# Weight casts of a feed-forward block moved from VectorE to GpSimd, on the queue that also issues the weight loads

## The reference

```python
def attn(x, Wq, Wk, Wv, Wo, gamma, beta):        # 16 heads of 64, causal
    q, k, v = projections of x
    out = softmax(mask(q @ k.T / 8)) @ v
    y = x + out @ Wo
    return layernorm(y, eps=1e-3) * gamma + beta
def ffn(x, w_gate, w_up, w_down):                # DIM 1024, HIDDEN 3072
    wg, wu, wd = w_gate / 127, w_up / 127, w_down / 127
    return (silu(x @ wg.T) * (x @ wu.T)) @ wd.T
x = x + attn(layernorm(x), ...)
x = x + ffn(layernorm(x), ...)                   # x: (16, 2048, 1024) float32
```

## Time and profile before

| what | us |
|---|---|
| median of 3 runs | 4214.85 (4174.06 to 4262.39) |
| time of the profiled execution | 4175.83 |
| its span, slowest core (core 3) | 4174.3 |
| spans of the 8 cores | 4146.8 to 4174.3 |
| mean granted TensorE clock of the cores | 0.839 to 0.845 of full speed |

### The profile page before, as it was taken

How to read it: one execution, slowest core, us unless ns; L and a number is a source line. 1 busy time by engine, 2 the same in 40 slices (tenths; PEclk the granted TensorE clock), 3 DMA queues, 4 the chain that set the end, 5 groups by cost and what they waited for, 6 DMA issues and landing times.

```text
span 4174.3 us, 44886 instructions; the slowest of 8 cores (4146.8 to 4174.3 us)
## 1 busy us (share of the span) xinstructions
PE 2608.2 (62%) x14352; PEld 1122.1 (27%) x14352; DVE 1751.8 (42%) x3199; ACT 1091.5 (26%) x1408; POOL 379.9 (9%) x644
## 2 busy tenths in 40 slices
PE   1455555587857567587714466465878574766877
PEld 0122222233323223233301223132333231332322
DVE  2533455444432441544435334544443325324543
ACT  0210325220036257110012103151100461661100
POOL 0000000022200000022300000000222000001222
PEclk6697678799979789799957976697999796898999
DMA  5102000076630000177741120001676200002776
GB/s 148 43 12 81 25 0 1 11 232 232 232 101 1 0 11 1 51 219 241 233 137 43 37 80 1 0 11 36 224 235 227 76 1 1 11 1 75 226 231 209
DMA packets 125732, 389.81 MB, mean 93 GB/s; under 512 B 14528, under 2 KB 14656, under 8 KB 125504
## 3 DMA queue, kind: packets, MB, share of 16 engines
q0 software_dynamic: 88064, 318.81, 23.4%
q1 hardware_dynamic: 37440, 68.12, 5.5%
HBM read 370.10 MB, written 16.78 MB: 93 GB/s over the span
## 4 chain that ended last, share of the span: by engine, by line
PE 27%; DMA 24%; DVE 21%; ACT 14%; issue 11%; SPq 1%; DVEq 1%; POOL 1%; ACTq 0%; POOLq 0%
ACT zr L711 9%; DMA wstag<-wu 8%; DMA wstag<-wd 6%; DMA wstag<-wg 5%; PE ps L588 3%; PE ps L520 3%; PE ps L326 2%; PE ps L693 2%; PE ps L770 2%; PE ps L476 2%; PE ps L666 2%; PE ps L957 2%; DMA xh<-x 2%; DVE zr L719 1%; PE ps L904 1%
## 5 line engine op out<-in xcount | busy, mean ns | idle before, releaser
L901 PE MATMUL ps<-zr,wgbb 128*128 128x512 bf16 x1536 | 601.3, 391 | 140.6 <-DVE wgbb L827 140.3
L711 ACT ACTIVATE zr<-ps,bbias 128x1024 bf16<-128x1024 f32 (+1 forms) x592 | 618.0, 1060 | 259.4 <-PE ps L696 212.2
L904 PE MATMUL ps<-zr,wubb 128*128 128x512 bf16 x1536 | 599.0, 390 | 109.1 <-DVE wubb L829 106.4
L666 PE MATMUL ps<-zr,vb 128*64 128x512 bf16 (+3 forms) x1280 | 378.4, 366 | 240.1 <-DVE zr L719 153.6
L818 POOL DMA_DIRECT2D wstag<-wu x192 | 119.2, 621 | 3142.0 <-DVE wgbb L827 3095.4
L957 PE MATMUL ps<-zr,wdbb 128*128 128x512 bf16 x1536 | 357.0, 386 | 74.1 <-DVE wdbb L948 72.3
L911 ACT ACTIVATE xst<-ps 128x512 bf16<-128x512 f32 x192 | 114.2, 597 | 1013.0 <-PE ps L901 878.0
L696 PE MATMUL ps<-qsb,kb 128*64 128x512 bf16 (+3 forms) x1280 | 371.5, 376 | 0.0
L693 PE MATMUL ps<-qsb,kb 128*64 128x512 bf16 (+3 forms) x1280 | 369.4, 374 | 0.0
L672 PE MATMUL ps<-zr,cbt 128*64 128x512 bf16 (+3 forms) x1280 | 358.4, 377 | 0.0
L719 DVE TENSOR_TENSOR zr<-zr,cbt 128x128 bf16<-128x128 bf16 x512 | 115.1, 225 | 485.0 <-ACT zr L711 414.5
(11 more groups left out here) (103 smaller groups left out, 3778.7 us busy)
## 6 DMA issues: line engine op xcount, KB each, us to landing
wstag<-wg POOLq DMA_DIRECT2D x192, 512.0 KB, 5.0
wstag<-wu POOLq DMA_DIRECT2D x192, 512.0 KB, 4.9
wstag<-wd POOLq DMA_DIRECT2D x192, 512.0 KB, 4.9
xh<-x SPq DMA_DIRECT2D x128, 256.0 KB, 6.9
o<-xh POOLq DMA_DIRECT2D x64, 256.0 KB, 3.4
tsc<-wk SPq DMA_DIRECT2D x32, 256.0 KB, 2.9
tsc<-wv SPq DMA_DIRECT2D x32, 256.0 KB, 2.7
tsc<-wq SPq DMA_DIRECT2D x32, 256.0 KB, 2.8
```

The costliest lines, as they stand in the source:

```text
L666: w=vsl, p=pap, st=first_av[ar0], tp=av_tp: t.matmul(d, w, p, start=st, stop=False, tile_position=tp, skip_group_check=True),
L711: E_("s", lambda s, d=pap, a=PSB[tslot2][:, 0:512 + n], b=bb: s.activation(d, a, ACT.Exp, bias=b, scale=0.125), reads=[bPS[2 * tslot2], bP ...
L901: E_("t", lambda t, dc=dc, w=wgsl, z=z3_ap[dc], d=PS[gB][:]: t.matmul(d, w, z, start=(dc == 0), stop=(dc == NDC - 1)), reads=[bWG[wsl], z3 ...
L904: E_("t", lambda t, dc=dc, w=wusl, z=z3_ap[dc], d=PS[uB][:]: t.matmul(d, w, z, start=(dc == 0), stop=(dc == NDC - 1)), reads=[bWU[wsl], z3 ...
```

## The change

All three casts go from VectorE's queue to GpSimd's. Shapes, buffers, order of recording and everything else stay. The lambdas of the down cast keep the name v for the engine they get.

```diff
@@ emit_guw_cast
-                    E_("v", lambda v, d=gb_, s=wstag[:, gsl * 1024:(gsl + 1) * 1024]: v.tensor_copy(d, s),
+                    E_("g", lambda g, d=gb_, s=wstag[:, gsl * 1024:(gsl + 1) * 1024]: g.tensor_copy(d, s),
                        reads=[bWST[gsl]], writes=[bWG[wsl]])
-                    E_("v", lambda v, d=ub_, s=wstag[:, usl * 1024:(usl + 1) * 1024]: v.tensor_copy(d, s),
+                    E_("g", lambda g, d=ub_, s=wstag[:, usl * 1024:(usl + 1) * 1024]: g.tensor_copy(d, s),
                        reads=[bWST[usl]], writes=[bWU[wsl]])
@@ down phase
-                        E_("v", lambda v, d=db_, a=stg: v.tensor_scalar(
+                        E_("g", lambda g, d=db_, a=stg: g.tensor_scalar(
                             d, a, 1.0 / 127.0, 0.0, AluOpType.mult, AluOpType.add),
                             reads=[bWST[sl], bCF], writes=[bWD[wsl]])
```

## The result

| | before | after |
|---|---|---|
| median, us | 4180.64 (4168.38 to 4274.58, 10 runs) | 4599.7 (4583.63 to 4623.81, 9 runs) |
| span of the profiled execution | 4174.3 (core 3) | 4597.8 (core 2) |
| spans of the cores | 4146.8 to 4174.3 | 4567.7 to 4597.8 |

The ratio of after to before is 1.1006, 95% interval 1.0983 to 1.103: the change costs 10%, some 420 us. The forecast was 13%, 4765 us in a range of 4590 to 5150; the measured time lies just inside its lower end. In some executions of every kernel here the cores of one half of the chip show a lower granted clock and the time is some per cent longer; such executions are in the medians and not in the ratios.

What follows compares the result with a forecast made beforehand. It took the three-slot ring of loads and casts to bound gate, up and down phases. Added: tf0 200, tf1 294, down 63, edges 15, together 572 over 4175.8, giving 4748, plus 17 for spread: 4765 us, range 4590 to 5150.

Steps and rivals of the forecast that it cites:

- The mechanism: Gate and up: casts waiting for tiles stand ahead of the next step's loads on GpSimd's queue, so loads lose their lead.
- The period: Gate and up: one step of two tiles takes 7.56 us, a sum along GpSimd's queue, against 4.4 measured before.
- The 0.50 from the end of cast u to the next issue: Gate and up: GpSimd issues the next load 0.50 us after cast u is done, one term of the period.
- landing of u: Gate and up: the load of wu takes 5.0 us from issue to landing, one term of the period.
- X: Duration of one cast on GpSimd, taken as 1.3 us, between a low end of 0.695 and a high end of 2.7.
- tf0 passes: Gate and up in tf0: 7.5 us, then 19 periods, 151.1 together; 50 more per pass, 200 for four.
- The down phase: Three loads stay ahead; cast and issue share GpSimd, 2.45 us per step against 2.11, 63 us more in all.
- TensorE's low clock: Gate and up: clock falls to 0.62, a step takes 6.8 us, hidden below 7.56 except 15 us at pass ends.
- The lock between VectorE and GpSimd: tf0 down phases: 16 normalizing VectorE instructions could hold up GpSimd casts, 11 us per pass, 44 in all, left in range.
- The slow cast: Rival: GpSimd's cast becomes the bound, X of 2 or more; about 5160 us at 2.1, 5470 at 2.7. Chance 0.22.
- Shorter landings: Rival: with less traffic u lands after 4.3 us, X is 1.0, period 6.8; about 4580 us. Chance 0.15.
- That GpSimd keeps its lead: Rival: loads issued in time despite casts, gate and up stays at 4.4 us per step, 4123 us total. Chance 0.03.

Runs made afterwards that it cites:

- e3: Against the changed kernel, only the load order differs: the load of tile n + 3 right behind the cast of tile n. 4238.43 us, ratio to before 1.0143.
- e4: Against the kernel before, casts still on VectorE, a step's loads wait for the second cast of the step before. Median 4691.45 us.
- e5: Against the changed kernel, each gate and up cast is done twice on GpSimd. 4968.22 us, ratio 1.1902.
- e2: Against the kernel before, only the down casts move to GpSimd. 4187.12 us, ratio 1.0029.
- e6: Against the changed kernel, weight loads are issued from SyncE, all casts staying on GpSimd. 4043.2 us, ratio to before 0.9687.
- e9: Against the kernel before, weight loads are issued from SyncE, casts staying on VectorE. Median 4087.52 us, ratio 0.9755.
- e1: Against the changed kernel, down casts are back on VectorE, so only gate and up casts are on GpSimd. 4571.95 us, ratio to before 1.0941.
- e8: Against the kernel before, loads convert int32 to bf16 themselves into a ring of 12 bf16 tiles, with no casts. 3924.73 us, ratio 0.9346.

## Why the prediction was right, and its terms

**The mechanism** was as put: the loads lose their lead in gate and up, the down phase keeps it, the period is a sum along GpSimd's queue. e3 and e4 show it from both sides, since the order alone takes the loss away and gives it without the change.

**The period** was forecast at 7.56 us and is 6.74 to 6.85 in the four tf1 passes. The step that failed is the sum 0.50 + 0.61 + landing of u + 0.16 + X (6.27 + X, not 6.26), in two terms:

- The 0.50 from the end of cast u to the next issue isn't there: cast u ends at 1126.20 and load g has started at 1126.15 by the rows above. I took it from the earlier trace rows, where it is the time from VectorE's cast to GpSimd's issue. In the new order load g waits for no cast of the pair just done: its slot was freed by the cast of wu one step earlier. The half microsecond does come back where a load waits for the cast right ahead of it, 0.56 in e3 and in the down phase.
- X was taken as 1.3 and is 1.05, ScalarE's rate for 1024 columns in the earlier trace rows, not that of L913. The Trainium skill ("GPSIMD Engine Reference", section 4.1) calls one-input operations roughly line-rate, by the prediction's estimate 0.85 us, and that is nearer to the measured 1.05 than the 1.54 from the 1.8 cycles of its section 3.1.

The rest held: issue to issue 0.53 (0.61 forecast), landing of wu 5.0 at the median (5.0), landing to cast 0.2 (0.16). With the measured values 0.53 + 5.0 + 0.2 + 1.04 = 6.77. Put in place of 7.56 it takes 0.79 x 168 = 133 from the sum of 572, the down phase another 35 and the edges 14, which leaves 390 against 397 measured in the passes.

**How much of the hit is luck.** With the right terms the passes give 182 us less than the forecast, and 27 us outside them, which no term of the prediction holds, bring the time back: without them it would be about 4573, below the range. So the mechanism was right, the size of the loss was forecast 1.4 times too large, and that the time falls just inside the range is partly luck. Of the signs, GpSimd's casts (1.05 us, not 1.1 to 1.6), the distance of cast u to cast u (6.7 to 6.9, not 7.0 to 8.1), the traffic (153 GB/s, not near 140) and VectorE's busy time (339 lower, not 400) all came out beside the forecast; for the last one the cause wasn't looked for.

**tf0 passes** take 134.9 to 141.4 us, forecast 151.1; 7.3 and 19 periods of 6.8 make 136.5. That GpSimd casts ahead and that TensorE does step 1 at once and then stops is in the trace: L913 of steps 0 and 1 stand together behind the epilogue.

```profile
843.56 0.69 DVE L810 TENSOR_TENSOR xh<-xh,tsc 128x512 f32<-128x512 f32 x1
844.17 0.42 DVE L340 CAST xst<-xh 128x512 bf16<-128x512 f32 x1
844.51 1.28 DVE L913 TENSOR_TENSOR zr<-xst,ps 128x512 bf16<-128x512 bf16 x2
```

**The down phase** was forecast at 2.45 per step and is 2.26 to 2.36. Cast and issue on one engine do set it, 1.06 + 0.56 + 0.58 = 2.20 at least; X was the term too large.

**TensorE's low clock** was forecast to be hidden, with 15 us at the edges. The granted clock in gate and up fell from 0.96 to 0.83 and 0.89, the matmuls' mean from 391 to 432 ns, and the edges lost 0.9 us in all. Hidden it was. The clock didn't fall to 0.62, and TensorE idles for a third of the period and not for over half of it: it is busy for 70% and 65% of the two stretches above. That also rules out TensorE as the bound, though a step at the 1.2 GHz level would take 6.8 us, as long as the measured period.

**The lock between VectorE and GpSimd** ("SBUF — State Buffer" in the Trainium skill) was left in the range with up to 44 us. The down phases with the normalizing instructions (tf0) sum to 213.3 us and those without (tf1) to 210.0; before, 197.4 and 197.9. The rule may be at work in these 3.8 us, and no run here isolates it.

**The rivals.** The slow cast (X of 2) fell with X = 1.05. Shorter landings came only for wg (4.2 at the median, it was 5.0), which doesn't set the period; wu needs 5.0, where it needed 4.9, though the traffic fell by a third. The measured time is near this rival's 4580 and the period near its 6.6 to 6.8, but by the missing half microsecond and not by its mechanism. That GpSimd keeps its lead fell, as its point of decision said: it needed a landing below 1.8.

**What stays open.** The 27 us outside the passes. On the mean of the eight cores the first epilogue ends 5.5 us later than before (639.1 against 633.6), while the cores of one execution spread over 9 to 14 us there; the stretch between the sequences is 19 longer on the profiled core by the two pages, which show different cores, 5 longer on the mean of the eight (832.9 against 828.0) and the same on core 3. The other two kernels that have all casts and all loads on GpSimd, e3 and e5, also spend 29 and 28 us more than before outside the passes on their profiled cores; e2, e4, e6 and e9 spend 10 to 16 less, and e1, whose down casts are on VectorE, 8 more. So it seems to come with the change; no run isolates its cause.

## What to carry to other kernels

On an engine that works strictly in order, an instruction that waits for a load must not stand ahead of the issue of the next loads: before moving work to an idle engine, list what that engine's queue issues and for whom. If casts must share the queue, issue load n + slots right behind cast n, or give the loads a queue that does nothing else. The same holds for stores that wait for a result. And where a ring of slots sets the pace, as the chain of waits shows by a load in every turn, look at the slots, at the length of a turn and at what the loads stand behind, here removed together by a load that converts on the way, and not at which engine casts.

## What the runs showed of the hardware

- GpSimd converts 128x1024 int32 to bf16 in 1.05 us, with or without a multiplication (1.048 and 1.060), against VectorE's 0.695.
- A load issued from GpSimd starts 0.5 us after the cast that it waits for, on VectorE (0.50, before and e4) or on GpSimd itself (0.56, e3); from SyncE 0.06 us after (e6). The landing of 512 KB, counted from the issue, is 4.7 to 5.0 us at the median from either.
- A load that converts int32 to bf16 keeps up: with 12 slots the steps of e8's first tf1 pass are 3.45 us apart, which is 1.05 MB read per step, 304 GB/s per core; between 1000 and 1090 us all eight cores are in such a stretch, at 156 to 171 GB/s of the bf16 side.
